# A mixer's decays through memory: one broadcast load for two heads in place of two spreading matmuls

## The reference

```python
zxbcdt = einsum('bld,ed->ble', u, in_proj_w)
z, xBC, dt = split(zxbcdt)                    # 1024, 1024+128+128, 16 heads
xBC = silu(conv4(xBC) + conv_b)               # x (16 heads x 64), B (128), C (128)
dt = softplus(dt + dt_bias); dA = exp(dt * -exp(A_log))
h  = h * dA_t + dt_t * outer(x_t, B_t)        # per head, over the 256 tokens
y  = h @ C_t + D * x
y  = rmsnorm(y * silu(z), ssm_norm_w) @ out_proj_w.T
```

## Time and profile before

| | before |
|---|---|
| median of 3 runs | 2830.31 us |
| the profiled execution's own time | 2830.18 us |
| its span | 2828.4 us |
| TensorE busy | 2701.0 us |
| VectorE busy | 1559.0 us |
| ScalarE busy | 1030.2 us |
| GpSimd busy | 571.5 us |
| DMA, mean over the span | 52 GB/s |

### The profile page before, as it was taken

How to read it: one execution, slowest core, us unless ns; L and a number is a source line. 1 busy time by engine, 2 the same in 40 slices (tenths; PEclk the granted TensorE clock), 3 DMA queues, 4 the chain that set the end, 5 groups by cost and what they waited for, 6 DMA issues and landing times.

```text
span 2828.4 us, 42157 instructions
## 1 busy us (share of the span) xinstructions
PE 2701.0 (95%) x15200; PEld 2089.0 (74%) x15200; DVE 1559.0 (55%) x2598; ACT 1030.2 (36%) x2385; POOL 571.5 (20%) x532
## 2 busy tenths in 40 slices
PE   6999999999999999999999999999999979999998
PEld 4777777777778888888888766777677757777775
DVE  6887797797785231232223577777777763211222
ACT  6244344334434122212221354555555543222221
POOL 0643543453361100101010012112121110000000
PEclk9999999999999999999999999999999989999999
DMA  4011001101114110111012210111101213211111
GB/s 133 16 46 45 19 25 44 44 0 44 45 45 135 60 45 15 59 59 59 0 59 93 90 46 11 57 52 59 59 7 59 78 46 119 75 59 44 44 44 45
DMA packets 85417, 147.81 MB, mean 52 GB/s; under 512 B 3968, under 2 KB 17920, under 8 KB 85344
## 3 DMA queue, kind: packets, MB, share of 16 engines
q1 hardware_dynamic: 85344, 146.84, 15.1%
HBM read 113.27 MB, written 33.55 MB: 52 GB/s over the span
## 4 chain that ended last, share of the span: by engine, by line
PE 84%; DVE 10%; issue 3%; ACT 2%; DMA 1%; DVEq 0%; POOL 0%; POOLq 0%; SPq 0%; ACTq 0%
PE ps L75 22%; PE ps L77 21%; PE ps L76 21%; PE ps L1639 4%; PE ps L1918 4%; PE ps L730 3%; PE ps L1651 2%; DVE mx_cv L537 2%; DVE at_pT L1502 1%; DVE mx_m L545 1%; PE ps L706 1%; DVE at_r L1491 1%; PE ps L1630 1%; PE ps L718 1%; PE ps L1659 1%
## 5 line engine op out<-in xcount | busy, mean ns | idle before, releaser
L1354 ACT ACTIVATE at_pr<-ps,at_nm 128x256 f32<-128x256 f32 x512 | 236.3, 474 | 221.2 <-DVE at_nm L1496 221.1
L1056 DVE TENSOR_TENSOR gm_m_lo<-gm_m,gm_m_hi 128x512 fp32r<-128x512 f32 (+1 forms) x88 | 62.1, 705 | 417.5 <-ACT gm_m_hi L973 417.5
L75 PE MATMUL ps<-sh_u_hi,gm_gu_hi 128*128 128x512 f32 (+1 forms) x704 | 274.7, 390 | 1.6 <-DVE gm_gu_lo L213 1.6
L76 PE MATMUL ps<-sh_u_lo,gm_gu_hi 128*128 128x512 f32 (+1 forms) x704 | 274.6, 390 | 0.0
L77 PE MATMUL ps<-sh_u_hi,gm_gu_lo 128*128 128x512 f32 (+1 forms) x704 | 274.5, 390 | 0.0
L1502 DVE COPY at_pT<-ps 128x512 f32<-128x512 f32 x256 | 176.3, 689 | 125.8 <-PE ps L1639 121.5
L967 ACT ACTIVATE gm_sg<-ps 128x512 f32<-128x512 f32 (+1 forms) x88 | 52.7, 598 | 519.1 <-PE ps L77 519.1
L1639 PE MATMUL ps<-sh_ident,at_pr 128*128 128x128 f32 x1024 | 167.2, 288 | 55.9 <-DVE at_pT L1502 51.8
L1639 PEld LDWEIGHTS ps<-sh_ident,at_pr 128*128 128x128 f32 x1024 | 120.9, 145 | 112.9 <-DVE at_pT L1502 40.8
L75 PE MATMUL ps<-sh_u_hi,qm_w_hi 128*128 128x512 f32 x512 | 200.7, 392 | 0.0
L77 PE MATMUL ps<-sh_u_hi,qm_w_lo 128*128 128x512 f32 x512 | 199.3, 389 | 0.0
(11 more groups left out here) (237 smaller groups left out, 6302.5 us busy)
## 6 DMA issues: line engine op xcount, KB each, us to landing
sh_xf<-x_scratch SPq DMA_DIRECT2D x16, 1024.0 KB, 7.5
sh_xf<-in_x SPq DMA_DIRECT2D x8, 1024.0 KB, 7.3
mx_xr<-in_x SPq DMA_DIRECT2D x8, 1024.0 KB, 5.9
h_scratch<-mx_xr SPq DMA_DIRECT2D x8, 1024.0 KB, 5.1
sh_xf<-h_scratch SPq DMA_DIRECT2D x8, 1024.0 KB, 8.2
gm_xr<-in_x SPq DMA_DIRECT2D x8, 1024.0 KB, 7.2
gm_r<-h_scratch SPq DMA_DIRECT2D x8, 1024.0 KB, 6.0
x_scratch<-gm_r SPq DMA_DIRECT2D x8, 1024.0 KB, 5.0
```

The costliest lines, as they stand in the source:

```text
L75: nc.tensor.matmul(out, l_hi, r_hi, start=first, stop=False)
L76: nc.tensor.matmul(out, l_hi, r_lo, start=False, stop=False)
L1354: A(pr[h][:, t, :], SC[h][:, SEQ * t:SEQ * t + SEQ], ACT.Exp, bias=nm[:, 4 * n + h, t:t + 1], accum_out=sums[:, 2 * b + t, 4 * g + h:4 * g ...
```

## The change

The decays are copied out of PSUM in fp32 as 16 rows (`daT`, L602 before), stored to a small tensor in HBM (`decay_scratch`, 32 KB), and loaded back two heads at a time with a broadcast over all 128 partitions (512 KB in SBUF), straight into the pair's two `m0` buffers. The two short scans of both heads (`second_scans`) read the decays there and write `m1`; then each head's long scan overwrites its decays with its mask in place. The eight loads wait on SyncE for `chunk_y` of two pairs before, where the scans waited before. The split into high and low parts, the selector `sel`, the 128 spreading matmuls and their waits go.

```diff
             sp.dma_start(xf[:, :, :], hs[0] if final(i) else xs[i + 1]).then_inc(s["xf"], 16)
-            if step_0(i):
-                sp.wait_ge(su.lo, wt.lows())
-            at(sp, s["st"], 16 * i)
-            sp.dma_start(xr[:, :, :], xs[i]).then_inc(s["xr"], 16)
+
+            sp.wait_ge(s["dac"], 3 * i + 3)
+            sp.dma_start(decays, daT[:, :]).then_inc(s["dw"], 16)
+            sp.wait_ge(s["dw"], 16 * i + 16)
+            for j in range(KI):
+
+                at(sp, s["y"], KI * i + j - 1)
+                sp.dma_start(m0[:, 2 * (j % 2):2 * (j % 2) + 2, :],
+                             decays[2 * j:2 * j + 2, :].partition_broadcast(P)).then_inc(s[f"db{j % 2}"], 16)
+                if j == 1:
+                    if step_0(i):
+                        sp.wait_ge(su.lo, wt.lows())
+                    at(sp, s["st"], 16 * i)
+                    sp.dma_start(xr[:, :, :], xs[i]).then_inc(s["xr"], 16)
...
         def scan(i, h):

-            dve.wait_ge(s["bc"], NH * i + h + 1)
-            at(dve, s["y"], KI * i + h // 2 - 1)
-            bank = BC[h % 2]
-            V.tensor_tensor_scan(m0[h % 4][:, :], bank[:, :], eye0[:, :], 0.0, ALU.mult, ALU.add)
-            V.tensor_tensor_scan(m1[h % 4][:, 0:P], bank[:, P:SEQ], ident[:, :], 0.0, ALU.mult, ALU.add)
-            V.tensor_tensor_scan(m1[h % 4][:, P:2 * P], bank[:, SEQ + P:2 * SEQ], ident[:, :], 0.0, ALU.mult,
-                                 ALU.add).then_inc(s["sc"], 1)
+            dve.wait_ge(s["s1"], NH * i + h + 1)
+            V.tensor_tensor_scan(m0[:, h % 4, :], m0[:, h % 4, :], eye0[:, :], 0.0, ALU.mult, ALU.add).then_inc(s["sc"], 1)
+
+        def second_scans(i, j):
+
+            dve.wait_ge(s[f"db{j % 2}"], 16 * (KI // 2 * i + j // 2 + 1))
+            for h in (2 * j, 2 * j + 1):
+                decay = m0[:, h % 4, :]
+                V.tensor_tensor_scan(m1[h % 4][:, 0:P], decay[:, P:SEQ], ident[:, :], 0.0, ALU.mult, ALU.add)
+                V.tensor_tensor_scan(m1[h % 4][:, P:2 * P], decay[:, SEQ + P:2 * SEQ], ident[:, :], 0.0, ALU.mult,
+                                     ALU.add).then_inc(s["s1"], 1)
...
-            dve.wait_ge(s["da"], i + 1)
-            V.tensor_copy(da_hl[:, :, 0:NH], d["da"]).then_inc(s["dah"], 1)
-            dve.wait_ge(s["dah"], i + 1)
-            V.tensor_tensor(da_hl[:, :, NH:2 * NH], d["da"], da_hl[:, :, 0:NH].bitcast(F32),
-                            ALU.subtract).then_inc(s["dal"], 1)
...
+            second_scans(i, 0)
             scan(i, 0)
             scan(i, 1)
...
             for j in range(KI):
                 if j + 1 < KI:
+                    second_scans(i, j + 1)
                     scan(i, 2 * j + 2)
...
-        def spread(i, h):
-
-            if h == 0:
-                if step_0(i):
-                    pe.wait_ge(su.dve, dve_0 + 8)
-                pe.wait_ge(s["dac"], 3 * i + 3)
-                pe.wait_ge(s["Ge"], 2 * i + 2)
-            elif h >= 2:
-                pe.wait_ge(s["sc"], NH * i + h - 1)
-            T.matmul(BC[h % 2][:, :], sel[:, h:h + 1].to_broadcast([P, P]), daT[:, :], start=True, stop=True).then_inc(s["bc"], 1)
...
             conv_in(i, NCONV - 2)
             z_in(i, 0)
-            spread(i, 0)
-            spread(i, 1)
             conv_in(i, NCONV - 1)
             turn_x(i, 0)
-            spread(i, 2)
-            spread(i, 3)
...
-                if j + 2 < KI:
-                    spread(i, 2 * j + 4)
-                    spread(i, 2 * j + 5)
```

More of the change, by code:

```diff
@@ L241, in tokens, with stage_mixer @@
     return ap.rearrange("(n t p) d -> n p t d", t=TT, p=P)
-def stage_mixer(nc, sem, su, sh, ps, x, h1, inp):
+def stage_mixer(nc, sem, su, sh, ps, x, h1, decays, inp):
     me = Stage()
-    smalls, dve_0 = su.stage(smalls=4, dves=9)
+    smalls, dve_0 = su.stage(smalls=3, dves=6)
     sb = Place(nc, "mx")
@@ L267, in stage_mixer @@
     sb.start(SEG[6])
-    m0 = [sb(f"m0_{r}", [P, NT]) for r in range(4)]
+    m0 = sb("m0", [P, 4, NT])
     m1 = [sb(f"m1_{r}", [P, NT // 2]) for r in range(4)]
@@ L310, in stage_mixer @@
                  lambda n: n % KI if n < IN_PIECES else KI + n % TT)
-    names = ("xr st dtp dtc dtt in G dat bc zp xt y out ss a nab ee u ln c rec c2 sp dt dta da dah dal "
+    names = ("xr st dtp dtc dtt in G dat dw db0 db1 s1 zp xt y out ss a nab ee u ln c rec c2 sp dt dta da "
              "dac tap cv sl Ge z xd sc M t g gs glo acc sse rg h1").split()
@@ L315, in stage_mixer @@
     me.s = s
-    def ahead(i):
-        return isinstance(i, int) and i == NP - 1
     CH = [8, 9] + list(range(KI))
@@ L332, in main @@
             sp.dma_start(xf[:, :, :], hs[0] if final(i) else xs[i + 1]).then_inc(s["xf"], 16)
-            if step_0(i):
-                sp.wait_ge(su.lo, wt.lows())
-            at(sp, s["st"], 16 * i)
-            sp.dma_start(xr[:, :, :], xs[i]).then_inc(s["xr"], 16)
+            sp.wait_ge(s["dac"], 3 * i + 3)
[10 more added lines that the diff above has]
+                    sp.dma_start(xr[:, :, :], xs[i]).then_inc(s["xr"], 16)
+                if final(i) and j == 1:
+                    sp.wait_ge(s["sl"], NCONV * NP)
+                    sp.wait_ge(s["G"], NP)
+                    me.nxt.wt.load(sp, 4)
+                elif final(i) and j == 5:
+                    sp.wait_ge(s["g"], KI * i + 4)
+                    me.nxt.wt.load(sp, 8)
             if final(i):
[L339 to L342, removed]
                 me.nxt.wt.load(sp, 12)
@@ L349, in sync @@
         sp.dma_start(ident[:, :], inp["ident"]).then_inc(su.small, 16)
-        sp.dma_start(sel_f[:, :], inp["sel"]).then_inc(su.small, 16)
         sp.dma_start(sh.post_w[:, :], inp["gm_cols"]).then_inc(su.small, 16)
@@ L379, in first @@
             act.wait_ge(su.small, smalls)
-            act.wait_ge(su.dve, dve_0 + 7)
+            act.wait_ge(su.dve, dve_0 + 5)
             A(a_neg[:, :, :], a_log, ACT.Exp).then_inc(su.act, 1)
@@ L600, in main @@
             dve.wait_ge(s["dat"], i + 1)
-            at(dve, s["bc"], NH * i)
-            V.tensor_copy(daT[0:2 * NH, :], Y[0:2 * NH, :]).then_inc(s["dac"], 1)
+            at(dve, s["dw"], 16 * i)
+            V.tensor_copy(daT[:, :], Y[0:NH, :]).then_inc(s["dac"], 1)
             dve.wait_ge(s["dac"], 3 * i + 1)
             for b in range(2):
-                V.memset(daT[0:2 * NH, SEQ * b:SEQ * b + 1].bitcast(F32), 0.0).then_inc(s["dac"], 1)
+                V.memset(daT[:, SEQ * b:SEQ * b + 1], 0.0).then_inc(s["dac"], 1)
             for n in range(4, NCONV - 1):
@@ L728, in chunk_y @@
                         h = 2 * j + hd
-                        m = m0[h % 4][:, SEQ * b:SEQ * b + SEQ] if blk == 0 else m1[h % 4][:, P * b:P * b + P]
+                        m = m0[:, h % 4, SEQ * b:SEQ * b + SEQ] if blk == 0 else m1[h % 4][:, P * b:P * b + P]
                         last = T.matmul(Y[HD * hd:HD * hd + HD, SEQ * b + P * blk:SEQ * b + SEQ],
@@ L762, in main @@
             at(pe, s["sse"], i)
-            pe.wait_ge(s["dal"], i + 1)
+            pe.wait_ge(s["da"], i + 1)
             for t in range(TT):
-                last = T.transpose(Y[0:2 * NH, P * t:P * t + P], da_hl[:, t, :].bitcast(F32), ident[:, :])
+                last = T.transpose(Y[0:NH, P * t:P * t + P], dts["da"][:, t, :], ident[:, :])
             last.then_inc(s["dat"], 1)
@@ L1934, in const_arrays @@
     zero = np.zeros_like(eye)
-    sel = np.concatenate([np.eye(NH, dtype=np.float32)] * 2)
     sel4 = np.concatenate([np.repeat(np.eye(AH, dtype=np.float32), AD, axis=1)] * 2)
     sel4 = np.concatenate([sel4, np.zeros((P - 2 * AH, HG * P), np.float32)])
-    return {"sel4": sel4, "qscale": np.full((P, 1), AD ** -0.5, np.float32), "ident": eye, "eye0": np.concatenate([eye, zero, eye, zero], axis=1), "sel": sel}
+    return {"sel4": sel4, "qscale": np.full((P, 1), AD ** -0.5, np.float32), "ident": eye, "eye0": np.concatenate([eye, zero, eye, zero], axis=1)}
 def build(nc, inp, out):
@@ L1950, in build @@
         x2 = nc.dram_tensor("x2_scratch", (TOK, DM), F32, kind="Internal").ap()
-        mx = stage_mixer(nc, sem, su, sh, ps, inp["x"], h1, inp)
+        decays = nc.dram_tensor("decay_scratch", (NH, NT), F32, kind="Internal").ap()
+        mx = stage_mixer(nc, sem, su, sh, ps, inp["x"], h1, decays, inp)
         gm = stage_gated_mlp(nc, sem, su, sh, ps, mx, inp["x"], h1, x1, inp)
```

17 lines of the change are left out of this document (4 added, 13 removed).

## The result

| | before | after |
|---|---|---|
| median of 4 runs | 2829.32 us | 2903.48 us |
| lowest to highest | 2826.48 to 2830.53 | 2898.71 to 2904.74 |
| ratio, 95% interval | | 1.026 (1.0247 to 1.0273) |
| the profiled execution's own time | 2830.18 us | 2903.34 us |
| its span | 2828.4 us | 2901.5 us |

What follows compares the result with a forecast made beforehand. TensorE bounds the pairs at 7.97 us; after the change VectorE's waits on GpSimd make them 9.5. Intervals +11.0 and tail 0.5 make 8 x 11.5 = +92 on 2830.18, so 2922 us, range 2885 to 2985.

Steps and rivals of the forecast that it cites:

- the exclusion: Scans with two SBUF inputs and GpSimd instructions wait for the whole of each other; 2922 us, chance 0.71.
- Rival A, no exclusion: Scans with two SBUF inputs do not exclude GpSimd, TensorE is nearly always fed; 2814 us, chance 0.10.
- The pair by hand: One pair of heads reckoned instruction by instruction on VectorE and GpSimd: 9.5 us instead of 7.97, lower bound 9.05.
- The four waits: VectorE's waits for GpSimd in one pair: 1.17, 0.61, 0.65 and 1.15, together 3.6 us.
- rival C, dear handovers: Exclusion with dear handovers, or consecutive scans passed ahead of waiting GpSimd: 10.4 us a pair, 2968 us, chance 0.15.
- The sum of intervals: Seven intervals between pairs' output matmuls in a step: 7.7 + 47.5 + 8.3 = 63.5 us against 52.5, so +11.0.
- The spreading matmuls: Their removal cuts a pair's TensorE work from 7.97 to 7.50 us, but the saving is hidden.
- The load: 512 KB loads of decays, eight a step, land in 3.8 us and stay hidden with 2 us spare.
- Rival B, late loads: No exclusion, but loads land after 5 us or more, some +2 a step; 2845 us, chance 0.04.
- TensorE's idle: TensorE idles some 2 us in each pair, released by VectorE or ScalarE.
- The means: Over the mixer the long scan's mean rises from 1.21 to about 1.8 us, the short ones' to about 0.8.
- The granted clock: TensorE's clock stays at 1.00 of 2.4 GHz in the pairs; a fall there would make the forecast wrong.

Runs made afterwards that it cites:

- the scans freed of exclusion: Changed kernel with the unit columns of all scans copied once a step into a free PSUM bank and read there: 2825.77 us against 2830.14, ratio 0.9986.
- few spreads: Kernel before without the 12 spreading matmuls a step inside the loop, later heads scanning what the banks hold: 2817.27 us, ratio 0.9956.

## Why the prediction was right, step by step

**What bounds it, and the exclusion: right.** VectorE became the bound through waits on GpSimd, and the operand place alone does it (2917 against 2829 us, no load, same order) and undoes it (2903 to 2826). Rival A, no exclusion, fell with the first scan of 2.28 us. But its price was too good: with the scans freed of exclusion the changed kernel takes 2825.8, not 2814. The first two intervals take 15.2 us there, or 16.0 with a low clock, against 14.9 before, so a middle step gains 1.0 or 1.7 us of the 3.8, and the loads are no longer covered.

**The pair by hand: 9.5 forecast, 9.16 measured.** Own work 5.96 against 5.93. The four waits 1.17, 0.61, 0.65 and 1.15 against 1.07, 0.49, 0.57 and 1.09, each at the forecast's place. The sum of 0.36 too much is that I put a gap at each change of holder; measured, the next one starts within some 0.05 us, and what remains is nearly the lower bound given (9.05). Of rival C, dear handovers, nothing was seen.

**The sum of intervals: +11.0 forecast, +8.45 measured.** First two 7.7 + 9.5 = 17.2 against 8.92 + 7.90 = 16.8; four pairs of 9.5 against 9.15 to 9.17, 1.4 less; the last 8.3 against 7.47: I had sized it 1.2 us shorter than a pair (two waits less), and it is 1.7 shorter. Tail +0.5 against +0.2. Per step +11.5 against +8.66, in all +92 against +74. The forecast of the loss was a quarter too large, 92 for 74, mostly from the handovers put into each pair and from the last interval. In the steps that the sum adds up it is 92 for 69; the 4 us in the last step and behind it were not in it, and that they bring the two numbers closer is luck.

**The spreading matmuls: right and without effect.** Their 3.8 us a step are hidden as forecast; freed of exclusion, pairs are 7.51 to 7.52 instead of 7.97.

**The load: right for this kernel.** 3.7 us to landing for 3.8, no wait in the middle pairs, 1.8 us to spare where 2 were forecast, and smaller loads gain no more than 1 us. Rival B, late loads, fell with that. The 2 us to spare were those of a pair of 9.2 us; at 7.5 there are none.

**TensorE's idle: right in size, 1.58 for some 2 us.** It names ScalarE, one of the two forecast.

**The means: too high.** The long scan's is 1.60 us where I wrote about 1.8, the short ones' 0.70 where I wrote about 0.8. The waits in a middle pair are as forecast, but I took every pair for a middle one: in two of a step's eight pairs no long scan is held up.

**The granted clock: not as forecast.** I wrote that it would stay at 1.00 in the pairs and that its fall would make the forecast wrong. In the middle pairs, with 1.6 us of idle time in each, it did stay there. But in the first interval it fell in every second step, behind the second of the two waits shown here and not behind the first (timeline, then windows, of two successive steps after, to be held against the earlier trace rows; the last window is middle pairs):

```profile
414.44 0.50 PE L75 MATMUL ps<-sh_u_hi,mx_wz_hi 128*128 128x512 f32 x1 [2.28 <-DVE mx_xdt L559]
...
525.24 0.50 PE L75 MATMUL ps<-sh_u_hi,mx_wz_hi 128*128 128x512 f32 x1 [2.27 <-DVE mx_xdt L559]
```

```profile
415.00:418.50 3.50, 3.48 (x23) 2.50 (x23) 3.50 (x6) 1.15 (x2) 2.42 (x2) 1.00 0.00 0
...
526.40:529.70 3.30, 3.30 (x9) 2.17 (x7) 3.30 (x5) 1.02 (x2) 1.80 (x2) 0.50 0.00 0
...
545.00:580.00 35.00, 28.67 (x171) 21.87 (x170) 35.00 (x40) 8.39 (x15) 26.12 (x20) 1.00 0.13 45
```

It cost nothing. In the step with the low clock the first two intervals are 8.92 and 7.90, together 16.82; in the step before (output matmuls at 410.06, 417.47 and 426.90) they are 7.41 and 9.43, together 16.84. VectorE, the bound, set both sums. So the term was missing from the forecast, but its value in this kernel is zero.

## What to carry to other kernels

Before an operand is moved from PSUM to SBUF, look whether a VectorE instruction then has both inputs in SBUF while GpSimd works there too: here the place of one operand, tried alone, cost 88 us, while the loads that the change adds and the matmuls that it removes counted for next to nothing. Such a wait is inside the durations, so compare means and longest values with the shortest, not idle times. Slack is that of the present period: when the bound goes away, a load that was covered by 2 us has to be reckoned anew.

## What the runs showed of the hardware that was not expected

- The exclusion passes from engine to engine within 0.05 us, and of four back-to-back short scans GpSimd's add, there at 564.18, got in before the fourth, which asked at 564.27. A 0.31 us scan pays 1.09 us for that.
- One operand in PSUM removes it fully: the longest of 128 long scans beside multiplies is 1.216 us.
- The second engine waits to the end of the other's instruction, however short its own is: a GpSimd multiply of 2 elements takes 1.11 us instead of 0.20 beside a long scan with two SBUF inputs.
- Waits of 1.84 to 2.39 us on TensorE were followed by about 3.4 us at 1.2 GHz in some steps and not in others (in the changed kernel and in the one with few spreads in every second one, behind the same waits of 2.27 and 1.9 us). Behind the mixer a wait of 1.63 us had it too (the kernel with few spreads, 843 us into the span), while six waits of 1.6 to 2.1 us in the changed kernel's last step, one a pair, had not. So the length of the single wait does not decide it; what does stays open. It costs 1.6 us where TensorE is the bound and nothing where VectorE is.
- The broadcast of 4 KB of HBM to 512 KB in SBUF lands in 3.7 us, as the plain load of 512 KB does; 64 KB take 2.0 us.
